# Causal attention scores of one batch row: two stretches of 384 columns for the two head pairs, in place of four blocks

## The reference, cut to what matters

```python
q = (x @ Wq).reshape(B, T, HEADS, HEAD_DIM).transpose(0, 2, 1, 3)
k = (x @ Wk).reshape(B, T, KV_GROUPS, HEAD_DIM).transpose(0, 2, 1, 3)
...
scores = jnp.einsum('bgptd,bgsd->bgpts', qg, k)
causal = jnp.triu(jnp.ones((T, T), bool), k=1)
scores = jnp.where(causal, -jnp.inf, scores)
weights = jax.nn.softmax(scores / jnp.sqrt(jnp.float32(HEAD_DIM)), axis=-1)
ctx = jnp.einsum('bgpts,bgsd->bgptd', weights, v)
...
x = x + _L0_attn_ref(_L0_cond_ref(x, L0_cond_weight, itok_B_3_7), ...)
x = x + _L0_ffn_ref(_L0_cond2_ref(x, itok_B_0_2, ...), ...)
```

## Time and profile before

| | |
|---|---|
| median of 3 runs | 237.53 us (237.14 to 239.57) |
| the profiled execution | 237.22 us, of which the instructions span 235.4 us |
| PE busy | 221.1 us (94%) |
| PE weight loads | 173.7 us (74%) |
| DVE busy | 172.3 us (73%) |
| ACT busy | 117.2 us (50%) |
| POOL busy | 96.2 us (41%) |
| chain that ended last | PE 77%, DVE 12%, ACT 4%, issue 2%, DMA 2% |
| natural scores on the chain (L1152) | 5% |
| maxima on the chain (L794) | 3% |

### The profile page before, as it was taken

The page is one execution under the profiler, slowest core; times in us unless marked ns, Lnnn a source line. Parts: engine busy times, 40 slices in busy tenths (PEclk is TensorE's granted clock), DMA queues, the critical chain, the costliest instruction groups (busy, mean ns, idle before and its releaser), DMA issues.

```text
span 235.4 us, 5807 instructions
## 1 busy us (share of the span) xinstructions
PE 221.1 (94%) x2010; PEld 173.7 (74%) x2010; DVE 172.3 (73%) x905; ACT 117.2 (50%) x287; POOL 96.2 (41%) x110
## 2 busy tenths in 40 slices
PE   6699997998999999999999999999999999899893
PEld 6588885786778876877687778777876776477693
DVE  0599838947864997589757975898489849948873
ACT  3697442686586257526752675266622650171210
POOL 7020570857369074707480748064922320002020
PEclk9999999999999999999999999999999999999999
DMA  4999508007002602260116011601101010003011
GB/s 131 319 387 361 202 1 277 6 0 226 3 3 56 225 3 58 55 213 4 57 52 218 4 56 47 223 3 57 45 3 47 13 45 3 0 4 102 0 47 45
DMA packets 20050, 21.18 MB, mean 90 GB/s; under 512 B 6453, under 2 KB 11573, under 8 KB 20021
## 3 DMA queue, kind: packets, MB, share of 16 engines
q1 hardware_dynamic: 20020, 20.81, 27.4%
HBM read 18.71 MB, written 2.10 MB: 88 GB/s over the span
## 4 chain that ended last, share of the span: by engine, by line
PE 77%; DVE 12%; ACT 4%; issue 2%; DMA 2%; SPq 1%; DVEq 0%; ACTq 0%
PE bank L1125 14%; PE bank L1126 12%; PE bank L1130 12%; PE bank L1152 5%; PE bank L1216 4%; PE bank L1178 4%; PE bank L1231 3%; PE bank L1136 3%; DVE thrown L794 3%; PE bank L1233 2%; PE bank L1232 2%; DMA stage_d<-base_t 2%; PE bank L1310 2%; ACT late L472 2%; DVE qkv_w_lo L724 2%
## 5 line engine op out<-in xcount | busy, mean ns | idle before, releaser
L373 POOL TENSOR_TENSOR cond_w_lo<-cond_raw,cond_w_hi 128x512 fp32r<-128x512 f32 x28 | 35.5, 1291 | 48.1 <-ACT cond_w_hi L472 48.1
L794 DVE CUSTOM_DVE_ANT_0 thrown<-bank,causal 128x64 f32<-128x64 f32 (+1 forms) x256 | 47.3, 253 | 0.6 <-issue 0.5
L393 POOL TENSOR_TENSOR rope_b<-rope_a,rope_b 128x128 f32<-128x128 f32 (+1 forms) x16 | 16.1, 1021 | 25.9 <-DVE rope_b L850 25.9
L472 ACT ACTIVATE max_rows<-bank,own_p 128x128 fp32r<-128x128 f32 x32 | 9.2, 369 | 33.3 <-PE bank L1162 33.3
L402 POOL TENSOR_TENSOR x_bias<-x,bias_row 128x512 f32<-128x512 f32 x8 | 10.3, 1290 | 28.7 <-DVE out_sb L974 27.3
L1125 PE MATMUL bank<-qkv_w_hi,c_t_hi 128*128 128x256 f32 (+1 forms) x64 | 21.4, 352 | 0.4 <-DVE c_t_lo L724 0.3
L1125 PE MATMUL bank<-fused_w_hi,late 128*128 128x324 f32 (+2 forms) x68 | 20.6, 318 | 0.9 <-ACT late L472 0.2
L794 DVE DVE_READ_ACCUMULATOR2_ANT neg_max<- 128x1 f32 x256 | 21.3, 83 | 0.0
L1126 PE MATMUL bank<-qkv_w_lo,c_t_hi 128*128 128x256 f32 (+1 forms) x64 | 20.3, 338 | 0.0
L1126 PE MATMUL bank<-fused_w_lo,late 128*128 128x324 f32 (+2 forms) x68 | 19.7, 306 | 0.0
L472 ACT ACTIVATE cond_w_hi<-cond_raw 128x512 fp32r<-128x512 f32 x32 | 17.5, 622 | 1.0 <-DMA cond_raw<-cond_w_t 1.0
(11 more groups left out here) (166 smaller groups left out, 631.4 us busy)
## 6 DMA issues: line engine op xcount, KB each, us to landing
cond_raw<-cond_w_t SPq DMA_DIRECT2D x7, 1024.0 KB, 5.5
xt_raw<-x_t SPq DMA_DIRECT2D x8, 256.0 KB, 5.9
x_nat<-x SPq DMA_DIRECT2D x8, 256.0 KB, 2.6
out<-out_sb SPq DMA_DIRECT2D x8, 256.0 KB, 2.0
stage_d<-base_t SPq DMA_DIRECT2D x4, 256.0 KB, 4.8
cond_raw<-cond_w_t SPq DMA_DIRECT2D x4, 256.0 KB, 4.6
stage_b<-w SPq DMA_DIRECT2D x4, 256.0 KB, 5.5
stage_a<-w_q SPq DMA_DIRECT2D x4, 256.0 KB, 5.9
```

The lines of the kernel that those rows point to most:

```text
L373: pool.tensor_tensor(cond_w.lo[:, k, :], cond_raw[:, k, :], f32(cond_w.hi[:, k, :]), ALU.subtract).then_inc(cond_lo, 1)
L393: pool.tensor_tensor(qk[:, at:at + w], rope_a[:, at:at + w], rope_b[:, at:at + w], ALU.add).then_inc(qk_ready, 1)
L472: return nc.scalar.activation(out, in_, ACT.Copy, scale=scale)
L794: nc.vector.tensor_tensor_reduce(thrown[:, b % 2, j, e, 0:width // 2] .rearrange("p (a s) -> p a s", a=h + 1), scores[:, :, e, :], causal[ ...
```

## The change

The blocks keep their numbers, shapes and matmuls. What differs is their order, their columns and where the calls stand.

- They are taken in turns 0, 2, 1, 3: first both blocks of head pair 0, then both of head pair 1.
- Columns: blocks 0 and 1 at 0 to 127, blocks 2 and 3 at 128 to 383. Each turn of two is a stretch of 384 columns, and the second stands in the same columns as the first.
- The late scores are now two blocks, 1 and 3. They wait for the maxima of blocks 0 and 2 (`maxed` at one half).
- The first maxima wait for two blocks, the last for all four.
- In every stage one block of 12 matmuls of 128 columns moves from the early to the late scores. On DVE, eight reductions over 128 columns move from before `split_hidden` and `split_c` to after `turn_context`, and the eight over 256 columns that stood between `split_hidden` and `split_c` now stand ahead of `split_hidden`.

```diff
-        block_at = (0, P, 2 * P, 0)
+        turns = (0, 2, 1, 3)
+        block_at = (0, 0, P, P)
         block_width = (P, P, 2 * P, 2 * P)
...
-            def maxima(t, b):
+            def maxima(t, i):
+                b = turns[i]
                 h, at, width = b // 2, block_at[b], block_width[b]
...
-                dve.wait_ge(scored, PER * t + max(b + 1, PER - 1))
-                if t > 0 or b > 1:
-                    dve.wait_ge(maxed, HEADS * t + 2 * PAIRS * (b - 1))
+                dve.wait_ge(scored, PER * t + (2 if i < 2 else PER))
+                if t > 0 or i > 1:
+                    dve.wait_ge(maxed, HEADS * t + 2 * PAIRS * (i - 1))
...
-            def score(t, b):
-                if b == 0:
+            def score(t, i):
+                b = turns[i]
+                if i == 0:
...
-                elif b == 3:
-                    pe.wait_ge(maxed, HEADS * t + 3 * HEADS // 4)
+                elif i == 2:
+                    pe.wait_ge(maxed, HEADS * t + HEADS // 2)
...
                 score(t, 0)
                 score(t, 1)
-                score(t, 2)
                 condition(f, range(2, KT))
...
                 context(r)
+                score(t, 2)
                 score(t, 3)
...
                 maxima(f, 0)
                 maxima(f, 1)
                 split_hidden(r)
-                maxima(f, 2)
                 split_c(g)
                 turn_context(t, 0)
                 turn_context(t, 1)
+                maxima(f, 2)
                 maxima(f, 3)
```

More of the change, by code:

```diff
@@ L781, in split_fused @@
                            ).then_inc(fused_lo, 1)
-            def maxima(t, b):
+            def maxima(t, i):
+                b = turns[i]
                 h, at, width = b // 2, block_at[b], block_width[b]
-                if t == 0 and b == 0:
+                if t == 0 and i == 0:
                     dve.wait_ge(tables_made, 3)
-                dve.wait_ge(scored, PER * t + max(b + 1, PER - 1))
-                if t > 0 or b > 1:
-                    dve.wait_ge(maxed, HEADS * t + 2 * PAIRS * (b - 1))
+                dve.wait_ge(scored, PER * t + (2 if i < 2 else PER))
+                if t > 0 or i > 1:
+                    dve.wait_ge(maxed, HEADS * t + 2 * PAIRS * (i - 1))
                 nc.vector.memset(waited[0:1, b:b + 1], 0.0)
@@ L793, in maxima @@
                     for e in range(2):
-                        nc.vector.tensor_tensor_reduce(thrown[:, b % 2, j, e, 0:width // 2]
+                        nc.vector.tensor_tensor_reduce(thrown[:, i % 2, j, e, 0:width // 2]
                                                        .rearrange("p (a s) -> p a s", a=h + 1),
@@ L1003, in _ @@
             split_fused(6)
-            maxima(0, 2)
             split_c(1)
             split_fused(7)
+            maxima(0, 2)
             maxima(0, 3)
@@ L1016, in _ @@
             maxima(1, 1)
-            maxima(1, 2)
             split_c(2)
@@ L1020, in _ @@
             turn_context(0, 1)
+            maxima(1, 2)
             maxima(1, 3)
@@ L1038, in _ @@
             split_hidden(0)
-            maxima(2, 2)
             split_c(3)
@@ L1042, in _ @@
             turn_context(1, 1)
+            maxima(2, 2)
             maxima(2, 3)
@@ L1083, in _ @@
             maxima(LAST, 1)
-            maxima(LAST, 2)
             turn_context(LAST - 1, 0)
             turn_context(LAST - 1, 1)
+            maxima(LAST, 2)
             maxima(LAST, 3)
@@ L1409, in _ @@
             score(0, 1)
-            score(0, 2)
             condition(1)
             transpose_c(1)
+            score(0, 2)
             score(0, 3)
@@ L1423, in _ @@
             score(1, 1)
-            score(1, 2)
             condition(2, range(2))
@@ L1428, in _ @@
             context(0)
+            score(1, 2)
             score(1, 3)
@@ L1486, in _ @@
             score(6, 1)
-            score(6, 2)
             condition(7, range(2, KT))
@@ L1494, in _ @@
             context(5)
+            score(6, 2)
             score(6, 3)
@@ L1516, in _ @@
             score(7, 1)
-            score(7, 2)
             keep_busy(6)
@@ L1521, in _ @@
             ffn_low_half(LAST - 2, 1, right_ps(LAST - 2))
+            score(7, 2)
             score(LAST, 3)
```

## The result

The changed kernel takes 245.29 us (median of 4 runs, 244.81 to 245.99), the kernel before 237.33 (4 runs, 236.84 to 239.57). The ratio is 1.032, with an interval of 1.028 to 1.036: slower by 8 us. The profiled execution took 244.81 us, of which the instructions span 243.0 (237.22 and 235.4 before).

A forecast was written before the change was run, and what follows sets the result against it. PE, busy 94% of the span at full clock, was taken as the bound, so only waits could move the time. Stage shifts of 3.15 + 0.86 + 1.07 + 0.63 + 0.58 + 0.6 = 6.9 gave 244.3 us, range 241.8 to 246.2.

The forecast's parts named there:

- Stages 3 to 5, 1.05 each: Transposed maxima on PE (L1162) start 1.05 us later per stage, 3.15 together, because `max_cols` on DVE comes later.
- `finish_ffn` 0.1 later, PE's 0.34 lost in a wait: At L1357, PE's 0.34 us from shorter early scores goes into waiting for `split_hidden`; L1357 comes 0.1 later.
- Stages 1 and 2, 0.63 and 0.86: At L1162, stage 1 adds 0.63 us, with no `finish_ffn` yet; stage 2 adds 0.86, with 0.4 off for L804.
- Stage 0, +0.6 and not -0.34: L1162 comes 0.6 us later as POOL's splits hold DVE's L804 and `max_cols`; without that hold, 0.34 sooner.
- Stage 6, 1.07: At L1162, 0.1 from the early part plus 1.16 of reductions less 0.19 of slack: 1.07 us later.
- Stage 7, 0.58: `context` ends 0.34 us sooner; with stage 3's DVE length from `turn_context` to `max_cols`, L1162 comes 0.58 later.
- That is the edge where the maxima meet PE.: PE's L1162 waits for DVE's `max_cols` (L806), 2.6 us in five stages; later DVE work ahead is paid by PE.
- The sum: Stage shifts at L1162 total 6.9 us, taking the profiled execution from 237.22 to 244.1 and the median to 244.3.
- the shift was not absorbed: Rival: PE or DVE catches up in half of the stages, 3.5 us remain, 241 us; chance 0.10.
- contention: Rival: L823 and L804 stay slow, 1.0 us more in stages 2 to 5; with later `finish_ffn`, 245.8; chance 0.12.
- the narrow reductions took their full step: Not-slower rival: `max_cols` is ready at L1162, for example if narrow reductions cost half their step; 236.9 us; chance 0.03.
- The clock rival: PE's clock falls to 1.2 GHz from `context` to L1162 in seven stages, costing 30 us: 267; chance 0.01.

The follow-up runs named there:

- The third experiment: The changed kernel with `split_hidden` moved ahead of the last two wide early reductions in stages 2 to 6: 243.24 us, ratio 1.023.
- the experiment on POOL: The changed kernel with POOL's last three adapter splits for stage 2 moved behind its two rotary additions: 245.01 us, ratio 1.031.
- the three experiments that relied on the first edge alone: `split_maxima` moved ahead of `scale_context` in the changed kernel, 246.26 us; in the kernel before, 238.02; in the changed kernel together with the `split_hidden` move, 243.67.
- the second edge's kernel: The kernel before with two unread 128x512 DVE additions between `split_maxima` and the second `scale_context` in stages 1 to 7: 244.52 us, ratio 1.031.
- the first experiment: The changed kernel with block 1 in its own columns, scored early, its maxima back ahead of `turn_context`, order 0, 2, 1, 3 kept: 237.77 us, ratio 1.003.
- The kernel with PE's part undone: The changed kernel with its DVE order kept, but block 1 in its own columns and scored early: 246.25 us, ratio 1.036.

## Why the prediction was right

The time came out at 245.29 where 244.3 was predicted, within 241.8 to 246.2, and slower as said. The steps, one by one:

- **Stages 3 to 5, 1.05 each**: 1.03, 1.05, 1.06. `context` starts 0.08 later relative to the stage's shift (109.94 - 2.30 - 107.56), `turn_context` 0.09 (0.1 said), the eight reductions cost 1.16, L825 fell from 0.63 to 0.42, and `max_cols` starts 1.04 later. PE's wait of 0.46 is less than the 0.6 said. That changes nothing: who is late is DVE.
- **`finish_ffn` 0.1 later, PE's 0.34 lost in a wait**: so it went, in a slightly other way. L1360 itself is on time (108.41 - 2.30 against 106.13), and the matmul behind it comes 0.25 later in place of 0.14. The third experiment shows the price of the wait as 0.43 a stage.
- **Stages 1 and 2, 0.63 and 0.86**: 0.67 and 0.87.
- **Stage 0, +0.6 and not -0.34**: 0.76, good to 0.3, by the hold that was named, and the experiment on POOL removed it. The Trainium skill (SBUF — State Buffer, "SBUF: two separate sides") has VectorE and GpSimd take turns at a shared pair of ports for a whole instruction; the trace agrees, 0.74 and 1.20 us beside POOL against 0.18 and 0.19 without it. The reductions, which read the banks, kept their step of 0.14 and 0.21 beside the same POOL instructions.
- **Stage 6, 1.07**: 1.18, 0.11 more than said. The term of the early part is too small there. I took 0.1 from stage 3, where DVE had waited 0.30 for ACT ahead of `split_hidden`. In stage 6 it had waited only 0.17 (rows below the list), so the longer early groups push `split_hidden`, `context` and `turn_context` back further: 0.23 against the stage's shift (185.48 - 5.44 - 179.81).
- **Stage 7, 0.58**: 1.01. This is the mis-sized term. I took DVE's length from stage 3, where the late scores directly follow `context`. In stage 7 `ffn_low_half` lies between, and DVE waits 0.32 for the scores behind `turn_context`. Moving them gave 0.37 back, most of the 0.43 that was missed. The program's order shows it; I had not checked when the new block's scores would be ready.
- **The step that was right in its number but incomplete**: "That is the edge where the maxima meet PE." There are two edges, `max_cols` at L1162 and the turned-back context at the output projection, with nearly no slack on either. For the change itself both give the same sum, since the eight reductions stand ahead of both. For anything built on it they do not: the three experiments that relied on the first edge alone missed by 4.4, 1.5 and 6.0 us.
- **The sum**: 6.9 predicted and 7.6 measured; 0.43 of the 0.7 is stage 7, 0.16 stage 0, 0.11 stage 6. For the median I added 0.3 to the profiled execution's 244.1, which is 244.4 and not the 244.3 that stands there; 0.48 was measured.
- **The rivals**: the shift was not absorbed (stage 0's stays to the end), contention gave way as reckoned, and the narrow reductions took their full step. The clock rival was put as 30 us in seven stages (its 267 is 237 and 30, without the shifts); of that nothing came in the profiled execution. A small form of it came in profiles of the experiments, in stage 7 alone.

The rows for stage 6: `split_hidden` and `turn_context` before, then `turn_context` in the changed kernel.

```profile
177.15 0.29 DVE L724 TENSOR_TENSOR late<-bank,late 128x128 fp32r<-128x128 f32 x1 [0.17 <-ACT late L472]
...
179.81 1.31 DVE L814 STREAM_TRANSPOSE turned<-bank 128x512 f32<-128x512 f32 x2
```

```profile
185.48 1.31 DVE L816 STREAM_TRANSPOSE turned<-bank 128x512 f32<-128x512 f32 x2 [1.70 <-PE bank L1219]
```

Between the profiled execution and the median lie 0.48 us. I put them down to the clock in stage 7, on the evidence below, but have no profile of the three longer executions (mean clock 0.992 to 0.993, spans 243.3 to 244.2). That they lost their time there is argued, not shown; one fall near 12 to 15 us gives the same mean (0.993 in the profile of the second edge's kernel).

None of these kernels is faster than the kernel before. The nearest are the first experiment and the change in stage 0 alone, both 237.77, and the kernel before with `split_maxima` moved, 238.02.

## What to carry to other kernels

Find the stretch of an engine that begins with something it must wait for and ends with something that the bottleneck waits for; work moved into it costs its length but for the slack, here 0.1 us, and the idle time that it leaves ahead of the stretch is worth nothing. Before a move is credited, follow the stretch to each of its readers, not only to the first: taking away the nearest wait gave nothing here, as the next one was 0.1 us behind. And where stages are written out apart, check each one's own order for when the moved work's inputs are ready.

## What was not expected of the hardware

**A low clock right behind a pause of 1.5 us or more, in some executions.** Seven kernels have a pause of 1.50 to 1.94 us ahead of L1165 in stage 7: the changed one and six experiments on it. Of their 28 executions 19 have a mean granted clock under 0.995. Of the kernels whose pause there is 0.97 or less (the kernel before and the other five), 21 of 83 have. Four of those seven kernels' profiled executions show 1.2 GHz for 3 to 4 us right behind the pause, and none of the six others' do. From L1165 or its counterpart to the end of the span these four take 32.1 to 32.4 us, and the changed kernel's profile 30.9. With the pause filled, no execution of six was low. The mean alone does not tell the place: four profiles show 0.50 near 12 to 15 us into the launch, one of them of a kernel without the long pause. Nor is the long pause shown to be the only cause of a costly fall. The kernel before has 11 executions of 43 under 0.995, and ten of them span 236.4 to 237.4 us, where the others span 234.9 to 236.1. None of them is profiled, and the falls near 12 to 15 us cost less than that where it can be read. The kernel with PE's part undone, with its pause of 1.93 us, in windows:

```profile
213.00:214.00 1.00, 1.00 (x20) 0.92 0.00 0
214.00:215.00 1.00, 0.87 (x7) 0.50 0.00 0
215.00:216.00 1.00, 1.00 (x3) 0.50 0.03 8
```

The Trainium skill (TensorE: Matmul & The Clock Gate, "A second HAM failure mode: psum-queue depth-cycling") tells of a kernel whose frequent short pauses between groups of matmuls made the clock swing. The traces agree only in part: in the changed kernel's profile the pauses of 0.45 to 0.47 in six stages, and the 1.94 in stage 7, left the clock at full speed, and in four other profiles it fell behind the long one.

**A short gap ahead of an instruction that reads what the reductions wrote.** With `split_maxima` directly behind the last reduction, L806 started 0.19 us after the start of the last accumulator read (114.60 to 114.79). The reciprocal that stood there in the changed kernel, which does not read the maxima, started together with it (both 114.79). The gap makes the move of `split_maxima` worse than nothing: DVE's run from `turn_context` to L833 grows by the 0.2 seen there. In stage 4 of the three kernels with this move, DVE waits 0.46 ahead of the instruction; the trace names only its own last reduction as what it waits for, and why it is longer there is open. That the dependence is the reason for the 0.19 is inferred; no experiment was made on it.
